# Two attentions on one Trainium2 core: where a step's eight value matmuls stand in TensorE's queue

## The chip, the cores and the metric

The kernel runs on one core of one Trainium2 chip. The metric is the device time of one execution in microseconds (us). A core has a matmul engine (PE, with its weight loads shown as PEld), a vector engine (DVE), a scalar engine (ACT), a general engine (POOL) and DMA queues, one of which is issued by SP. Each engine works through its own queue in the order written; between engines only semaphores order the work.

## The reference

What is computed is a chain of two blocks over x (2 batches, 1024 tokens, 128 channels). The change touches the two attentions with 16 heads of 8 channels over 1024 keys:

```python
attn = jnp.einsum('bhnd,bhmd->bhnm', q, k) * scale      # block 0
attn = jax.nn.softmax(attn, axis=-1)
attn_out = jnp.einsum('bhnm,bhmd->bhnd', attn, v)
...
p = jax.nn.softmax(qk, axis=-1)                          # block 1
mask = jnp.triu(jnp.ones((s, s), dtype=p.dtype), k=0)
p = p * mask
z = jnp.einsum('bhqk,bhkd->bhqd', p, v)
```

In block 1 the mask stands behind the softmax, so all 1024 keys count in the sum, and the masked probabilities are only left out of the product with v. Between and behind the attentions stand two windowed attention layers with their feed-forward parts, and a mixture of four experts run for four rounds; these are not touched.

## The kernel before

**Tiling.** One function, `attention` (L578), does both attentions; `causal` is False for block 0 and True for block 1. The 32 pairs of batch and head are worked on as 8 units of 4 heads. A unit has 2 halves of 512 queries, and a half has 8 steps, one for each tile of 128 keys: `LAST` = 128 steps `g` in each attention. In a step four heads are scored: `score` (L733) is a matmul of 50 rows by 512 queries into one of **three** PSUM banks (`st_bank[e % 3]`, L738 waits for the exponential three scores back); ACT takes the exponential of each into `probs` (L811, four buffers of four heads). `values` (L743) multiplies the four `probs` tiles of a step with v: four fp32 matmuls (L757), which the trace shows as eight instructions, into one bank over eight steps. It waits first for the last exponential of its step (L746).

**Maxima.** The softmax needs the largest score of each query before its scores are made. So 11 steps ahead (`LEAD`), `maximum` (L703) makes the same products with queries on the partitions, two matmuls of 512 into a ring slot of two banks, and DVE takes the maximum of the slot (L822). A step carries two such maxima, in four matmuls. There are two ring slots; slot n waits (`claim`, L698) until DVE is through with entry n-2. A score and the maximum matmul behind it use different halves of the PE's rows and run beside each other.

**Extras.** Once in eight steps the ring takes one more entry of each of two kinds. `rows` (L717, steps with g % 8 = 5) turns sixteen finished maxima to rows, which DVE casts (L837) after having split them (L827, L829) and SP writes into the operands. `turn` (L726, steps with g % 8 = 1, from g = 9) transposes the finished sums of a half. Before it, in the same step, ACT copies the value bank out (`take_sums`, L801 to L803) behind the step's first exponential, and the `values` of a half's first tile (issued in that same step) waits for this copy (L750). One extra entry changes which of the two slots the next maximum gets.

**Causal part.** In block 1 the key tiles that the diagonal crosses (64 of 128 steps: tiles 0 to 3 of the first half of a unit, 4 to 7 of the second) also need `probs` times a triangle. POOL makes it (`mask`, L889, L898) once the step's last exponential is done, and `values` ends with matmuls over it (L766) that wait for POOL (L763). Columns beyond the diagonal go by L760 instead of L757.

**The order of a step on PE** is written out by hand in L784 to L795. With S for a score, M0a, M0b, M1a, M1b for the four matmuls of the two maxima, and V for the values of the step before:

S0 M0a S1 M0b S2 M1a S3 M1b V extras

In the first 117 steps all of it is there; the last 11 have no maxima.

Of the kernel before, what the change touches and what calls it, by code (L numbers as in the profile page):

```python
# [577 lines left out]
def attention(nc, k, tag, scale, causal, operands, pool_aside=None):  # L578
# [23 lines left out]
    with ctx:  # L602
# [20 lines left out]
        def entries(g):  # L623

            out = []
            pair = g + LEAD
            if pair < LAST:
                out += [("max", 2 * pair), ("max", 2 * pair + 1)]  # L630
            if pair % SEQ_TILES == 0 and pair // SEQ_TILES - 1 < HALVES:
                out.append(("rows", pair // SEQ_TILES - 1))
            if g % SEQ_TILES == 1 and g > SEQ_TILES:
                out.append(("turn", g // SEQ_TILES - 1))
            return out
# [61 lines left out]
        def _(pe):  # L697
# [5 lines left out]
            def maximum(m, half):  # L703
                it, p, j, t = max_at(m)
                if half == 0:
                    buf = claim(("max", m))
                    if m % (2 * STEPS) == 0:
                        pe.wait_ge(loaded[it % RING], 16 * 4 * (it // RING + 1))
                buf = ring[number["max", m] % 2]
                mm = pe.matmul(buf[:, half * CHUNK:(half + 1) * CHUNK],  # L710
                               q_op[it % RING][at_rows(p, MAX_ROW), j, t * P:(t + 1) * P],
                               k_op[it % RING][at_rows(p, MAX_ROW), j, half * CHUNK:(half + 1) * CHUNK],
                               start=True, stop=True)
                if half:
                    mm.then_inc(ring_ready, 1)
# [17 lines left out]
            def score(g, i):  # L733
                it, half, t = g // STEPS, g // SEQ_TILES % 2, g % SEQ_TILES
                h = heads_of(g)[i]
                e, p, j = GROUP * g + i, h % 2, h // 2
                if e >= 3:
                    pe.wait_ge(exp_done, e - 2)  # L738
                pe.matmul(st_bank[e % 3], k_op[it % RING][at_rows(p, MAX_ROW + 2), j, t * P:(t + 1) * P],  # L739
                          q_op[it % RING][at_rows(p, MAX_ROW + 2), j, half * CHUNK:(half + 1) * CHUNK],  # L740
                          start=True, stop=True).then_inc(st_ready, 1)

            def values(g):  # L743
                it, half, t = g // STEPS, g // SEQ_TILES % 2, g % SEQ_TILES
                r = it % RING
                pe.wait_ge(exp_done, GROUP * (g + 1))  # L746
                if g % STEPS == 0:
                    pe.wait_ge(v_staged, it + 1)
                if t == 0 and g:
                    pe.wait_ge(evacuated, g // SEQ_TILES)  # L750
                first_tile, final = t == 0, t == SEQ_TILES - 1
                full = CHUNK if not causal else min(max(t - 4 * half, 0) * P, CHUNK)
                for j in range(GROUP):
                    out = out_bank[32 * j:32 * j + 32, :]
                    pr = probs[:, g % PB, j, :]
                    if full:
                        last = pe.matmul(out[:, 0:full], stage_v[r][:, t, j, :], pr[:, 0:full],  # L757
                                         start=first_tile, stop=final and full == CHUNK, skip_group_check=causal)
                    if full < CHUNK:
                        last = pe.matmul(out[:, full:CHUNK], only_ones[:, :], pr[:, full:CHUNK],  # L760
                                         start=first_tile, stop=final, skip_group_check=causal)
                if causal and 0 <= t - 4 * half < 4:
                    pe.wait_ge(masked, it * SEQ_TILES + t + 1)  # L763
                    at = (t - 4 * half) * P
                    for j in range(GROUP):
                        last = pe.matmul(out_bank[32 * j:32 * j + 32, at:at + P], stage_vo[r][:, t, j, :],  # L766
                                         diag[:, t % 2, j, :], start=False, stop=final, skip_group_check=True)
                last.then_inc(pv_done, 1)

            def extras(found):  # L770
                for kind, arg in found:
                    if kind == "rows":
                        rows(arg)
                    if kind == "turn":
                        turn(arg)
# [8 lines left out]
            for g in range(LAST):  # L784
                it, half = g // STEPS, g // SEQ_TILES % 2
                if g % SEQ_TILES == 0:
                    pe.wait_ge(m_rows[half], 32 * (it + 1))
                pair = g + LEAD
                for i in range(GROUP):
                    score(g, i)  # L790
                    if pair < LAST:
                        maximum(2 * pair + i // 2, i % 2)
                if g:
                    values(g - 1)
                extras(entries(g))  # L795
            values(LAST - 1)
            turn(HALVES - 1)
# [1259 lines left out]
```

## Time and profile before

| what | value |
|---|---|
| median of 3 runs | 1954.28 us (1953.3 to 1956.46) |
| the profiled execution | 1954.34 us |
| its span, first to last instruction | 1952.6 us |
| mean granted TensorE clock | 0.901 |
| PE busy | 1605.0 us (82%) |
| DVE busy | 1407.1 us (72%) |
| ACT busy | 1129.6 us (58%) |
| POOL busy | 604.3 us (31%) |
| exponentials L811 | 1024, 535.2 us, 602 ns each |
| maxima L822 | 512, 600.8 us, 1219 ns each |
| exponentials of block 0 | from 129.8 us to 461 us |
| exponentials of block 1 | to 1440 us |

The profiled execution is as good as the median. Busy time is a union of what the trace shows of an engine; a matmul's row shows about 0.38 us from its start to its modelled end, although the next one can start 0.22 us behind it, so PE looks busier than it is. For an order of queues the starts of instructions tell more than the busy shares: the prediction works from the starts.

### The profile page before, as it was taken

To read this page: it belongs to the slowest core of one execution; us is meant where nothing else is said; L and a number is where in the kernel's file an instruction comes from. 1 tells how busy PE (TensorE), PEld (TensorE's weight loads), DVE (VectorE), ACT (ScalarE), POOL (GpSimd) and SP (SyncE) were. 2 spreads that over 40 slices of the span, in tenths; PEclk is the share of its full clock that TensorE was granted. 3 is DMA by queue.
4 is the path that set the end of the run, shared out by engine and by line. 5 is a ranking of instruction groups with operands and counts; after the bars stand their busy time and mean duration, and the time that the engine had idled before them with its cause. 6 is when DMAs were issued, how large, how long until landed. Compare 5 with 4: busy or idle time off the path is not lost. (4 is left out here: it accounts for less than half of the span.)

```text
span 1952.6 us, 29634 instructions
## 1 busy us (share of the span) xinstructions
PE 1605.0 (82%) x11120; PEld 874.2 (45%) x11120; DVE 1407.1 (72%) x2091; ACT 1129.6 (58%) x2178; POOL 604.3 (31%) x494
## 2 busy tenths in 40 slices
PE   6279999997578885888771999999965998989997
PEld 4012222223356653566540233333324776767775
DVE  3499999992766456664443999999925787869787
ACT  3228888885466733667341477777742554545454
POOL 2550000001566424564002122222211353535354
PEclk8659999998699986899885799999987898989899
DMA  2410001001011100111004001110011000000000
GB/s 69 145 34 18 18 18 28 7 1 47 28 23 29 26 19 23 29 29 26 1 5 163 17 18 21 24 36 5 4 28 49 1 1 0 0 0 0 0 0 21
DMA packets 56776, 49.14 MB, mean 25 GB/s; under 512 B 37800, under 2 KB 41256, under 8 KB 56016
## 3 DMA queue, kind: packets, MB, share of 16 engines
q1 hardware_dynamic: 56016, 45.29, 8.8%
q10 hardware_dynamic: 576, 2.16, 0.3%
q8 instruction: 78, 1.28, 0.3%
q14 instruction: 42, 0.34, 0.1%
q0 software_dynamic: 64, 0.07, 0.0%
HBM read 24.34 MB, written 14.68 MB: 20 GB/s over the span
## 5 line engine op out<-in xcount | busy, mean ns | idle before, releaser
L811 ACT ACTIVATE att_probs<-psum 128x512 f32<-128x512 f32 x1024 | 535.2, 602 | 214.4 <-PE psum L739 213.7
L822 DVE TENSOR_REDUCE att_neg_max<-psum 128x1 f32<-128x1024 f32 x512 | 600.8, 1219 | 77.2 <-PE psum L710 71.4
L710 PE MATMUL psum<-att_k_op,att_q_op 48*128 48x512 bf16 x1024 | 350.9, 409 | 89.2 <-PEq L370 67.7
L739 PE MATMUL psum<-att_q_op,att_k_op 50*128 50x512 bf16 x1024 | 314.0, 387 | 19.2 <-ACT att_probs L811 19.0
L1831 ACT ACTIVATE moe_hidden<-psum,moe_b 128x512 f32<-128x512 f32 x256 | 168.9, 690 | 136.6 <-PE psum L76 116.1
L757 PE MATMUL psum<-att_probs,att_v 128*32 128x512 f32 (+2 forms) x1664 | 203.1, 558 | 2.9 <-ACT att_sums L803 2.8
L739 PEld LDWEIGHTS psum<-att_q_op,att_k_op 50*128 50x128 bf16 x1024 | 78.2, 94 | 250.8 <-ACT att_probs L811 187.6
L64 DVE CAST moe_hidden_high<-moe_hidden 128x512 fp32r<-128x512 f32 x256 | 149.0, 599 | 41.7 <-ACT moe_hidden L1831 41.7
L1860 POOL TENSOR_TENSOR moe_hidden_low<-moe_hidden,moe_hidden_high 128x512 fp32r<-128x512 f32 x64 | 107.0, 1672 | 203.3 <-DVE moe_hidden_high L64 203.3
L710 PEld LDWEIGHTS psum<-att_k_op,att_q_op 48*128 48x128 bf16 x1024 | 72.6, 95 | 213.7 <-DVE att_neg_max L822 120.7
L898 POOL TENSOR_TENSOR att_diag<-att_probs,att_triangle 128x512 f32<-128x512 f32 x64 | 81.4, 1272 | 269.0 <-PE psum L760 176.7
L69 DVE TENSOR_TENSOR moe_hidden_low<-moe_hidden,moe_hidden_high 128x512 fp32r<-128x512 f32 x192 | 130.4, 679 | 0.0
L74 PE MATMUL psum<-moe_cur_high,moe_w_high 128*128 128x512 f32 x256 | 107.5, 420 | 27.6 <-PEq L136 13.8
L1378 DVE TENSOR_REDUCE wl_mx<-psum 128x4 f32<-128x512 f32 x64 | 44.0, 688 | 116.1 <-PE psum L1179 116.1
L1296 ACT ACTIVATE wl_pr<-psum,wl_mx 128x128 f32<-128x128 f32 x256 | 73.2, 368 | 87.8 <-DVE wl_mx L1378 87.7
L1427 POOL TENSOR_TENSOR wl_qk<-wl_qk,wl_part 128x512 f32<-128x512 f32 x64 | 81.5, 1275 | 111.2 <-DVE wl_part L1361 111.1
L74 PE MATMUL psum<-moe_hidden_high,moe_w_high 128*128 128x512 f32 x256 | 112.5, 439 | 0.0
L75 PE MATMUL psum<-moe_cur_low,moe_w_high 128*128 128x512 f32 x256 | 105.5, 412 | 0.0
L76 PE MATMUL psum<-moe_cur_high,moe_w_low 128*128 128x512 f32 x256 | 105.5, 412 | 0.0
L76 PE MATMUL psum<-moe_hidden_high,moe_w_low 128*128 128x512 f32 x256 | 100.5, 393 | 0.0
L75 PE MATMUL psum<-moe_hidden_low,moe_w_high 128*128 128x512 f32 x256 | 99.9, 390 | 0.0
L1854 POOL TENSOR_TENSOR moe_cur<-moe_cur,moe_term 128x512 f32<-128x512 f32 x64 | 86.5, 1352 | 24.9 <-DVE moe_term L1923 24.1
(235 smaller groups left out, 2857.7 us busy)
## 6 DMA issues: line engine op xcount, KB each, us to landing
wl_v_shift<-wl_v SPq DMA_DIRECT2D x62, 128.0 KB, 2.3
att_q_op<-qk_parts SPq DMA_DIRECT2D x32, 192.0 KB, 3.2
att_k_op<-qk_parts SPq DMA_DIRECT2D x32, 192.0 KB, 4.2
qk_parts<-rot_hi SPq DMA_DIRECT2D x12, 256.0 KB
qk_parts<-plain_hi SPq DMA_DIRECT2D x12, 256.0 KB
qk_parts<-rot_mid SPq DMA_DIRECT2D x8, 256.0 KB
qk_parts<-plain_mid SPq DMA_DIRECT2D x8, 256.0 KB
moe_w<-in_moe_w SPq DMA_DIRECT2D x2, 1024.0 KB, 6.2
```

The lines of the kernel that those rows point to most:

```text
L64: return dve.tensor_copy(dst, src)
L69: return dve.tensor_tensor(dst, src, high.bitcast(F32), ALU.subtract)
L74: pe.matmul(out, w_high, x_high, start=start, stop=False)
L75: pe.matmul(out, w_high, x_low, start=False, stop=False)
L76: return pe.matmul(out, w_low, x_high, start=False, stop=stop)
L710: mm = pe.matmul(buf[:, half * CHUNK:(half + 1) * CHUNK], q_op[it % RING][at_rows(p, MAX_ROW), j, t * P:(t + 1) * P], k_op[it % RING][at_r ...
L739: pe.matmul(st_bank[e % 3], k_op[it % RING][at_rows(p, MAX_ROW + 2), j, t * P:(t + 1) * P], q_op[it % RING][at_rows(p, MAX_ROW + 2), j, ha ...
L757: last = pe.matmul(out[:, 0:full], stage_v[r][:, t, j, :], pr[:, 0:full], start=first_tile, stop=final and full == CHUNK, skip_group_check ...
L811: act.activation(probs[:, g % PB, h, :], st_bank[e % 3], ACT.Exp, scale=scale).then_inc(exp_done, 1)
L822: dve.tensor_reduce(neg[:, t, p, j:j + 1], ring[e % 2], AX.X, ALU.max, negate=True).then_inc(ring_free, 1)
L1831: act.activation(hidden[:, n % 2, f, :], k.psum[:, f, :], ACT.Gelu_apprx_tanh, bias=b1[:, e, f:f + 1]).then_inc(gelu_done, 1)
L1860: pool.tensor_tensor(hidden_low[:, n % 2, f, :], hidden[:, n % 2, f, :], hidden_high[:, n % 2, f, :].bitcast(F32), ALU.subtract).then_inc( ...
```

## The change

The `values` of the step before are issued behind the second score and its maximum matmul, instead of behind the fourth. Nothing else is changed; every wait, buffer and instruction is the same.

```diff
@@ -790,8 +790,8 @@
                     score(g, i)
                     if pair < LAST:
                         maximum(2 * pair + i // 2, i % 2)
-                if g:
-                    values(g - 1)
+                    if i == 1 and g:
+                        values(g - 1)
                 extras(entries(g))
             values(LAST - 1)
             turn(HALVES - 1)
```

The order of a step on PE is then: S0 M0a S1 M0b V S2 M1a S3 M1b extras. As the function is shared, it holds for both attentions.

## Rows read from the trace of the kernel before

**Rows 1.** The page, part 2: granted clock in 40 slices of the span.

```profile
PEclk8659999998699986899885799999987898989899
```

**Rows 2.** Busy by stretch: PE, PEld, DVE, ACT, POOL (instructions); clock, DMA share, GB/s.

```profile
290.00:310.00 20.00, 19.30 (x133) 4.94 (x134) 19.43 (x20) 16.55 (x33) 0.40 (x1) 1.00 0.16 41
```

**Rows 3.** Timeline of ACT, block 0: start, length, instructions, [idle before].

```profile
299.79 0.60 ACT L811 ACTIVATE att_probs<-psum 128x512 f32<-128x512 f32 x1 [0.33 <-PE psum L739]
300.28 0.59 ACT L803 ACTIVATE att_sums<-psum 128x512 f32<-128x512 f32 x1
...
303.02 2.06 ACT L811 ACTIVATE att_probs<-psum 128x512 f32<-128x512 f32 x4 [0.68 <-PE psum L739]
305.42 2.07 ACT L811 ACTIVATE att_probs<-psum 128x512 f32<-128x512 f32 x4 [0.33 <-PE psum L739]
307.81 2.06 ACT L811 ACTIVATE att_probs<-psum 128x512 f32<-128x512 f32 x4 [0.33 <-PE psum L739]
310.20 2.06 ACT L811 ACTIVATE att_probs<-psum 128x512 f32<-128x512 f32 x4 [0.33 <-PE psum L739]
...
318.17 2.06 ACT L811 ACTIVATE att_probs<-psum 128x512 f32<-128x512 f32 x4 [0.40 <-PE psum L739]
```

**Rows 4.** Timeline of PE, block 0, a step without extras.

```profile
306.07 0.39 PE L739 MATMUL psum<-att_q_op,att_k_op 50*128 50x512 bf16 x1
...
306.39 1.06 PE L757 MATMUL psum<-att_probs,att_v 128*32 128x512 f32 x8
307.39 0.39 PE L739 MATMUL psum<-att_q_op,att_k_op 50*128 50x512 bf16 x1
...
307.62 0.38 PE L710 MATMUL psum<-att_k_op,att_q_op 48*128 48x512 bf16 x1
...
308.08 0.39 PE L710 MATMUL psum<-att_k_op,att_q_op 48*128 48x512 bf16 x1
```

**Rows 5.** Timeline of DVE in the same step.

```profile
306.81 1.22 DVE L822 TENSOR_REDUCE att_neg_max<-psum 128x1 f32<-128x1024 f32 x1
...
308.06 2.36 DVE L822 TENSOR_REDUCE att_neg_max<-psum 128x1 f32<-128x1024 f32 x2
```

**Rows 6.** Timeline at block 0's end: last two exponentials, then the last values.

```profile
460.76 1.09 ACT L811 ACTIVATE att_probs<-psum 128x512 f32<-128x512 f32 x2
461.90 0.16 PEld L757 LDWEIGHTS psum<-att_probs,att_v 128*32 128x32 f32 x8 [0.99 <-ACT att_probs L811]
```

**Rows 7.** Timeline of PE, block 0: values in a turn step.

```profile
301.02 0.64 PE L757 MATMUL psum<-att_probs,att_v 128*32 128x512 f32 x4 [0.19 <-ACT att_sums L803]
```

**Rows 8.** Timeline of PE, block 0: M0a in the step behind a rows step.

```profile
313.16 0.39 PE L710 MATMUL psum<-att_k_op,att_q_op 48*128 48x512 bf16 x1 [0.40 <-DVE att_neg_max L822]
```

**Rows 9.** Timeline of PE, block 1: values with a diagonal part, then S0.

```profile
1269.07 0.87 PE L757 MATMUL psum<-att_probs,att_v 128*32 128x384 f32 x8
...
1269.96 0.42 PE L766 MATMUL psum<-att_diag,att_v 128*32 128x128 f32 x8
1270.31 0.39 PE L739 MATMUL psum<-att_q_op,att_k_op 50*128 50x512 bf16 x1
```

**Rows 10.** Timeline of ACT, block 1.

```profile
1266.43 1.09 ACT L811 ACTIVATE att_probs<-psum 128x512 f32<-128x512 f32 x2
...
1276.83 2.06 ACT L811 ACTIVATE att_probs<-psum 128x512 f32<-128x512 f32 x4 [0.57 <-PE psum L739]
1279.47 2.06 ACT L811 ACTIVATE att_probs<-psum 128x512 f32<-128x512 f32 x4 [0.57 <-PE psum L739]
```

**Rows 11.** Timeline of POOL, block 1: two of its 64 masks.

```profile
1267.61 1.28 POOL L898 TENSOR_TENSOR att_diag<-att_probs,att_triangle 128x512 f32<-128x512 f32 x1 [1.55 <-ACT att_probs L811]
...
1440.26 1.28 POOL L898 TENSOR_TENSOR att_diag<-att_probs,att_triangle 128x512 f32<-128x512 f32 x1 [1.37 <-ACT att_probs L811]
```

**Rows 12.** Timeline of PE, end of block 1: diagonal matmuls that wait for the mask.

```profile
1441.60 0.32 PE L766 MATMUL psum<-att_diag,att_v 128*32 128x128 f32 x4 [0.27 <-POOL att_diag L898]
```

**Rows 13.** Timeline of PE early in block 0, at the lower clock.

```profile
133.99 1.93 PE L757 MATMUL psum<-att_probs,att_v 128*32 128x512 f32 x8
```

## The prediction, made before the changed kernel was built

> **What bounds the kernel now.** I read the busy time by stretch first. In a stretch of block 0, DVE is busy 19.43 of 20 us and PE 19.30, ACT only 16.55 [rows 2]. By these shares DVE or PE is the bound and the order of PE's queue hardly matters. Then I read the starts, and they say something else. ACT begins a step of four exponentials every 2.39 us (305.42, 307.81, 310.20) and stands idle 0.33 us before each, waiting for a score [rows 3]. On PE, S3 starts at 306.07, V at 306.39, the next step's S0 at 307.39 [rows 4]. The chain that fills the period is: exponential 0 starts 305.42; S3 needs its bank (three banks) and starts 0.65 us later; V is queued behind S3 and M1b, 0.32 later; V holds the queue 1.00; S0 to its exponential takes 0.42 (307.39 to 307.81). 0.65 + 0.32 + 1.00 + 0.42 = 2.39. That is a **loop between ACT and PE**, and each link is a row. DVE does not close it: two of its maxima start 1.25 us apart where it had to wait for M0b (306.81, 308.06; M0b started at 307.62, 0.44 us earlier [rows 4]), while two that do not wait stand 1.14 apart (2.36 for two, less one length of 1.22 [rows 5]).
>
> **What the change does to a plain step.** Nothing is added or removed; V moves past S2, M1a, S3 and M1b. No DMA and no other queue's order moves. V's own wait, for exponential 3 of the step before, was long met when V came last; now it stands where it counts. S1 starts when exponential 2 of the step before has given its bank back. V could follow M0b by 0.32, but exponential 3 ends 0.48 after exponential 2 (four start within 2.06 less one length of 0.62, so 0.48 apart [rows 3]), so V always waits for ACT, about 0.15 us. Behind V stand S2 and S3. So the new loop is: exponential 3 starts; V starts 0.65 later (its length 0.60 and a hand-over of 0.05: the pair of exponentials that begins at 460.76 ends at 461.85, V's weights load at 461.90 [rows 6]); V holds PE 1.00 [rows 4]; S2 to exponential 2 takes 0.42 [rows 4, 3]; the next exponential starts 0.49 behind one that came late (299.79 to 300.28 [rows 3]). 0.65 + 1.00 + 0.42 + 0.49 = **2.56 us, 0.17 more than 2.39**. The old loop with V's wait taken out would be 0.65 + 0.32 + 1.00 + 0.42 = 2.39 again, so even a free wait gains nothing: V stands in front of two scores in place of four, yet ACT has only two in hand in place of three. The steps without maxima have the same loop. 128 steps in each block: +21.8 us in each.
>
> **A turn step (g % 8 = 1).** V now waits in mid-step for ACT's copy of the sums, which stands behind exponential 0. From the start T of exponential 3: exponential 0 at T + 0.48, the copy at T + 0.97, V 0.73 behind the copy's start (300.28 [rows 3], 301.02 [rows 7]), so T + 1.70 in place of T + 0.65: +1.05. The step is 3.61.
>
> **The step behind it.** One extra entry shifts the ring, so that M0a of the next step needs the slot that M1 of the turn step filled. M1b used to come before V, and its maximum was taken under V's 1.00 us. Now M1b is last, and only the extra and S0 stand between it and M0a. From M1b: 0.44 to DVE's start, 1.27 from there to the slot's release (306.81 [rows 5] to M1a at 308.08 [rows 4]), 0.22 to M0b, 0.32 to V: V starts 2.25 behind M1b. In a plain step M1b stands 1.87 behind T and the next V 2.56 + 0.65 behind T, 1.34 apart. So V loses another 0.92. That such a wait happens at all is seen today behind a rows step (0.40 us on DVE before M0a [rows 8]). The two steps together pay 1.05 + 0.92 = 1.97 for a turn. Today it costs 303.02 - 299.79 = 3.23, less 2.39, 0.84 [rows 3]. Net +1.12 for 15 turns in block 0, less 0.9 for the last, which has no maxima behind it: +15.9 us.
>
> **A rows step (g % 8 = 5).** The same slot wait falls on the step behind it: 0.92. The matmuls of `rows` themselves lie under it. Today three steps from 310.20 to 318.17 take 7.97 in place of 7.17: 0.80 [rows 3]. Net +0.12, 15 times: +1.8 us. DVE's load stays under it: 97% of 20.76 us (8 x 2.39 + 0.84 + 0.80), 20.2 us, in eight steps that now take 23.4 (8 x 2.56 + 1.97 + 0.92).
>
> Block 0: 21.8 + 15.9 + 1.8 = **39.5 us**.
>
> **Block 1, the mask.** In 64 steps V carries a diagonal part that waits for POOL. Today V comes so late that the mask is ready (POOL begins 1267.61, ends 1268.89 [rows 11]; the diagonal matmuls start 1269.96 [rows 9]). Such a step takes 2.64 now (1276.83 to 1279.47 [rows 10]). After: exponential 3 ends T + 0.60; POOL begins 0.08 later (1267.53, the end of the two exponentials [rows 10], to 1267.61) and takes 1.28; the hand-over to PE is 0.05 (1441.54 to 1441.60 [rows 11, 12]): T + 2.02. V's first part, begun at T + 0.65, takes 0.89 [rows 9] and is done at T + 1.54, so PE stands 0.48 us behind POOL. Then 0.35 of diagonal matmuls (1269.96 to 1270.31), 0.42 and 0.49 as above: **3.28 in place of 2.64, +0.64**. 64 x 0.64 = 41.0. The 64 others: 64 x 0.17 = 10.9. The extras in units' plain halves go as in block 0: 8 x (1.12 + 0.12) less 0.9 = 9.0. Those in diagonal steps I take at nothing: the late copy (V at T + 1.70) and the slot wait lie mostly under the mask wait (T + 2.02); if that cover is gone they cost up to 14 x 1 us more, and as they already cost up to 0.8 each today they could also give 5 back. Block 1: **60.9 us**.
>
> **Sum.** 39.5 + 60.9 = 100.4 us on the profiled execution's 1954.34, which stands at the median (1954.28): 2055 us. A difference of about 0.2% is what a measurement of this kernel can tell from no change. The terms I cannot read are bounded so. V's start behind a waited exponential: 0.05 after the end [rows 6], at most 0.14, as behind the copy (0.73 less 0.59 [rows 7, 3]); I take the first, which is the same wait; the other end adds 0.09 x 190, 17 us. The slot wait: 0.92 computed, none at best; it stands on some 42 steps (39 us) in the sum, and I take it whole as rows 8 show its kind; half of it is 19 us.
>
> **Rivals.** (a) **DVE sets the pace**: its work is unchanged, it is busy 97% [rows 2], so nothing changes: 1954. Against it: DVE's starts 1.25 apart where 1.14 is possible [rows 5], and the loop that adds up. The Trainium skill (Perfetto Trace Analysis, "Identifying the Most-Contended Engine") calls the engine with the highest occupancy the one to look at first; by that this would be the case, but the rows' starts disagree. 5%. (b) **Faster**: the extras (0.84 and 0.80 a half) come earlier against DVE, since rows and turns no longer queue behind V, and the step falls to DVE's floor, 20.2 us a half in place of 20.76; over 30 halves 17 us: 1937. It decides if V's wait for ACT is met on arrival and M1b's maximum is out of the slot before M0a. The first fails by 0.15, the second by 0.9 us. 4%. (c) **Only the mask hurts less**: POOL's 1.28 is covered after all and block 1 loses 0.17 a step: 100.4 - 64 x 0.47 = 70 us: 2025. For it: nothing but that other stalls can overlap. 6%. (d) **The clock falls**: in attention the granted clock is 1.00 [rows 2] (2.4 GHz); the page's slices show it lower elsewhere [rows 1]. At the lower level V is 1.93 in place of 1.06 long [rows 13, 4]; with that alone a step grows by 0.87, 256 steps 223 us: 2280. For it: PE gets new waits each step. Against: they are 0.15 to 0.5 us, and today's waits before S3 and M1a are like them at a clock of 1.00. The Trainium skill (TensorE: Matmul & The Clock Gate, "A second HAM failure mode: psum-queue depth-cycling") tells of a kernel where short idle times between groups of matmuls made the clock go up and down; this trace does not agree, its attention steps have such gaps and stay at 1.00. 2%.
>
> **Numbers.** My forecast 83%: 2055, its own range by the bounds 2055 - 19 - 5 to 2055 + 17: 2031 to 2072. The low end goes down to (c), the high end takes in a few of the 14 us of lost cover: 2025 to 2075. Faster 0.04, same 0.05, slower 0.91.
>
> **What would show it.** ACT's starts 2.56 apart in plain steps of block 0, with an idle of 0.5 before exponential 2 and not before exponential 0; V's weights waiting on L811; a turn pair 3.6 and 3.5 long; in block 1 L766 waiting about 0.48 on L898 in most of 64 steps, steps of 3.28; DVE no longer nearly full. It would be wrong if steps stay 2.39 (V's wait met), if M0a behind extras does not wait, or if the clock in the attentions is under 1.00.

## The result and the profile after

The changed kernel takes 2063.72 us (median of 4 runs, 2060.4 to 2064.29) where the kernel before took 1955.37 us beside it (1953.3 to 1959.49). The ratio is 1.0548, with a 95% interval of 1.0526 to 1.0569: **slower by 5.5%, some 108 us**. Forecast were 2055 us and a range of 2025 to 2075. All times and ratios here are of undisturbed executions; one of e6's four, at 2980.2 us, was a slow one and is left out.

The page of the changed kernel, in its parts 1, 2 and 5 (busy us, mean ns of one, then idle time before the group and what ended most of it):

```profile
span 2062.5 us, 29606 instructions
...
PE 1604.9 (78%) x11092; PEld 861.3 (42%) x11120; DVE 1413.4 (69%) x2091; ACT 1140.8 (55%) x2178; POOL 604.8 (29%) x494
...
PEclk9569999998589996999975899999997799999999
...
L822 DVE TENSOR_REDUCE att_neg_max<-psum 128x1 f32<-128x1024 f32 x512 | 608.2, 1220 | 182.2 <-PE psum L710 179.1
L811 ACT ACTIVATE att_probs<-psum 128x512 f32<-128x512 f32 x1024 | 546.6, 603 | 311.0 <-PE psum L739 309.6
```

The work is the same: PE busy 1604.9 us (1605.0 before), one exponential 603 ns (602), one maximum 1220 ns (1219). (ACT's busy time still shows 11 us more, 1140.8 for 1129.6: exponentials that follow without a wait start 0.48 us apart and are 0.60 long, so their rows overlap, and fewer now do.) What grew is waiting. ACT now stands idle 311.0 us in front of its exponentials, 214.4 before, and in nearly all of it for a score. DVE, which looked full, waits 182.2 us for maximum matmuls, 77.2 before.

The same stretch of block 0 as in [rows 2], by stretch (PE, PEld, DVE, ACT, POOL, then the clock):

```profile
290.00:310.00 20.00, 16.83 (x119) 4.27 (x119) 16.86 (x17) 14.61 (x29) 0.00 (x0) 1.00 0.01 1
```

PE and DVE fell from 97% to 84% together, at a clock of 1.00. So neither sets the pace of the changed kernel. That DVE did not set it before either is not shown by this; e11 below shows it.

ACT's timeline in block 0, changed kernel (start, length; a group of four now begins with a step's exponential 2, in front of which ACT waits):

```profile
304.11 2.07 ACT L811 ACTIVATE att_probs<-psum 128x512 f32<-128x512 f32 x4 [0.92 <-PE psum L739]
306.68 2.07 ACT L811 ACTIVATE att_probs<-psum 128x512 f32<-128x512 f32 x4 [0.49 <-PE psum L739]
309.24 2.07 ACT L811 ACTIVATE att_probs<-psum 128x512 f32<-128x512 f32 x4 [0.49 <-PE psum L739]
...
315.40 2.07 ACT L811 ACTIVATE att_probs<-psum 128x512 f32<-128x512 f32 x4 [0.92 <-PE psum L739]
...
320.53 1.58 ACT L811 ACTIVATE att_probs<-psum 128x512 f32<-128x512 f32 x3 [0.49 <-PE psum L739]
...
327.65 2.07 ACT L811 ACTIVATE att_probs<-psum 128x512 f32<-128x512 f32 x4 [0.92 <-PE psum L739]
```

304.11 to 306.68 to 309.24: a plain step is **2.56 us**, 2.39 before [rows 3]. A rows step and the next are 6.16 (309.24 to 315.40), a turn's two steps 7.12 (320.53 to 327.65).

PE's timeline in a plain step, changed kernel:

```profile
316.06 0.39 PE L739 MATMUL psum<-att_q_op,att_k_op 50*128 50x512 bf16 x1 [0.25 <-ACT att_probs L811]
...
316.55 1.06 PE L757 MATMUL psum<-att_probs,att_v 128*32 128x512 f32 x8
317.54 0.39 PE L739 MATMUL psum<-att_q_op,att_k_op 50*128 50x512 bf16 x1
...
319.11 1.06 PE L757 MATMUL psum<-att_probs,att_v 128*32 128x512 f32 x8
```

S1 at 316.06, V at 316.55, which is 0.49 later and not the 0.32 at which a V can follow (the rest is the wait for exponential 3), S2 at 317.54, the next V 2.56 behind. In the answer on waits for 150 to 470 us, V's weights waiting for ACT, 5.5 us in 150 to 430 us before, now stand high (third line: total us, times, longest):

```profile
PEld psum L739 <- ACT att_probs L811: 135.2, 205, 0.8
ACT att_probs L811 <- PE psum L739: 82.5, 149, 1.1
PEld psum L757 <- ACT att_probs L811: 58.3, 109, 1.4
```

Block 1, a diagonal step of the changed kernel, PE, POOL and ACT:

```profile
1290.57 0.66 PE L757 MATMUL psum<-att_probs,att_v 128*32 128x256 f32 x8
...
1291.95 0.43 PE L766 MATMUL psum<-att_diag,att_v 128*32 128x128 f32 x8 [0.28 <-POOL att_diag L898]
1292.30 0.39 PE L739 MATMUL psum<-att_q_op,att_k_op 50*128 50x512 bf16 x1
```

```profile
1290.59 1.30 POOL L898 TENSOR_TENSOR att_diag<-att_probs,att_triangle 128x512 f32<-128x512 f32 x1 [2.66 <-ACT att_probs L811]
```

```profile
1289.43 2.07 ACT L811 ACTIVATE att_probs<-psum 128x512 f32<-128x512 f32 x4 [1.17 <-PE psum L739]
1292.73 2.07 ACT L811 ACTIVATE att_probs<-psum 128x512 f32<-128x512 f32 x4 [1.23 <-PE psum L739]
```

V and the mask begin at the same time (1290.57, 1290.59); the mask ends at 1291.89 and the diagonal matmuls follow at 1291.95. The step is 3.30 us (1289.43 to 1292.73), 2.64 before [rows 10].

Between the starts of the first and the last exponential, the trace has block 0 at 374.3 us (331.4 before) and block 1 at 410.7 us (346.6 before): +42.9 and +64.1. What lies between the blocks took 3.3 us more in the profiled pair, although nothing changed there; over all the runs below it lies between 626.5 and 638.7 us (631.7 in the profile of before), so this is scatter. The kernel before itself, timed 13 times beside e4 to e6 and e8, gave 1949 to 1964 us.

### The profile page after: what moved, and what is told of

Its sections match the earlier page's. It is cut to its first block and busy times, and to the rows that moved or that the text cites. A ratio compares the mean times of both kernels' runs of the same rounds, so it can differ in the third digit from the quotient of the medians.

```text
span 2062.5 us, 29606 instructions
## 1 busy us (share of the span) xinstructions
PE 1604.9 (78%) x11092; PEld 861.3 (42%) x11120; DVE 1413.4 (69%) x2091; ACT 1140.8 (55%) x2178; POOL 604.8 (29%) x494
## 3 DMA queue, kind: packets, MB, share of 16 engines
q8 instruction: 78, 1.28, 0.3%
## 5 line engine op out<-in xcount | busy, mean ns | idle before, releaser
L822 DVE TENSOR_REDUCE att_neg_max<-psum 128x1 f32<-128x1024 f32 x512 | 608.2, 1220 | 182.2 <-PE psum L710 179.1
L811 ACT ACTIVATE att_probs<-psum 128x512 f32<-128x512 f32 x1024 | 546.6, 603 | 311.0 <-PE psum L739 309.6
L710 PE MATMUL psum<-att_k_op,att_q_op 48*128 48x512 bf16 x1024 | 335.7, 407 | 103.2 <-PEq L370 69.6
L739 PE MATMUL psum<-att_q_op,att_k_op 50*128 50x512 bf16 x1024 | 318.8, 388 | 44.5 <-ACT att_probs L811 44.4
L76 PE MATMUL psum<-moe_hidden_high,moe_w_low 128*128 128x512 f32 x256 | 100.4, 392 | 0.0
L760 PE MATMUL psum<-att_probs,att_only_ones 128*32 128x512 f32 (+3 forms) x768 | 84.1, 504 | 19.9 <-ACT att_sums L803 17.6
```

The lines of the kernel that those rows point to most:

```text
L76: return pe.matmul(out, w_low, x_high, start=False, stop=stop)
L710: mm = pe.matmul(buf[:, half * CHUNK:(half + 1) * CHUNK], q_op[it % RING][at_rows(p, MAX_ROW), j, t * P:(t + 1) * P], k_op[it % RING][at_r ...
L811: act.activation(probs[:, g % PB, h, :], st_bank[e % 3], ACT.Exp, scale=scale).then_inc(exp_done, 1)
L822: dve.tensor_reduce(neg[:, t, p, j:j + 1], ring[e % 2], AX.X, ALU.max, negate=True).then_inc(ring_free, 1)
```

## The experiments

The diffs show the lines that matter, against the kernel before; e10's is against e4. Block times are those between first and last exponential in the profiled execution; totals are medians. The ratios are estimates against executions of before made beside each run (medians 1955.3 to 1959.4 us) and need not be the quotient of two numbers of this table.

| run | block 0 | block 1 | total | ratio to before (95%) |
|---|---|---|---|---|
| before | 331.4 | 346.6 | 1955 to 1959 | 1 |
| changed | 374.3 | 410.7 | 2063.7 | 1.0548 (1.0526, 1.0569) |
| e1 block 0 only | 372.3 | 346.6 | 2000.5 | 1.0218 (1.0181, 1.0256) |
| e2 block 1 only | 331.6 | 409.5 | 2019.6 | 1.0315 (1.0275, 1.0354) |
| e3 lag two | 362.7 | 382.4 | 2027.9 | 1.0355 (1.0316, 1.0394) |
| e4 behind S0 | 455.9 | 499.8 | 2241.5 | 1.1465 (1.1396, 1.1535) |
| e5 behind S2, M1a | 404.8 | 416.5 | 2095.1 | 1.0708 (1.0668, 1.0748) |
| e6 extras behind V | 361.3 | 404.7 | 2043.6 | 1.0462 (1.0409, 1.0516) |
| e7 diagonal late | 372.3 | 382.2 | 2037.2 | 1.0420 (1.0383, 1.0458) |
| e8 before, diagonal split | 332.1 | 340.0 | 1949.8 | 0.9964 (0.9944, 0.9983) |
| e9 behind S2, before M1a | 361.5 | 384.6 | 2027.5 | 1.0363 (1.0327, 1.0399) |
| e10 e4 with filler | 457.6 | 498.4 | 2231.4 | 1.1389 (1.1353, 1.1425) |
| e11 values in halves | 317.8 | 342.2 | 1941.4 | 0.9922 (0.9898, 0.9946) |

**e1 and e2: one block at a time.** The values stand at `i == 1` in one block and last in the other.

```diff
-                if g:
+                    if i == 1 and g and not causal:   # e2: and causal
+                        values(g - 1)
+                if g and causal:                      # e2: and not causal
                     values(g - 1)
```

> Only block 0's attention has the values behind the second score; block 1 has the old order. My theory (each block's loop stands alone): block 0's exponentials take 374 us in place of 331, block 1 keeps its 374, the total is about 43 us over before, near 1998 us; the two one-block runs together give the whole change. Rival (something outside the attentions, such as the clock or the layers between, takes part): the two do not add up to 108 us, or a one-block run gains or loses in the other block.

> Only block 1's attention has the new order. My theory: block 1's exponentials take 438 us in place of 374, block 0 keeps 331, the total is about 64 us over before, near 2019 us. Rival: as for the block 0 run, the parts do not add up.

Measured: 45 us over before with block 0 alone, 64 with block 1 alone by the medians, together 109; by the ratios 43 and 62, together 104, each known to some 8 us. The whole change costs 107 to 108. The unchanged block keeps its time to 0.2 us in both. So the two costs stand apart and add up within what can be measured. (The 374 us that the expectations give block 1 before is not the 346.6 of the table; what they forecast is the differences, 43 and 64, and the block times show 41 and 63.)

**e3: the same place, but nothing to wait for.** The values are those of two steps before, the copy of the sums and the turns come one step later.

```diff
-                if g:
-                    values(g - 1)
+                    if i == 1 and g >= 2:
+                        values(g - 2)
...
+            values(LAST - 2)
             values(LAST - 1)
```

> The values stand in the new place but are those of two steps before (copy of the sums and turns one step later), so their wait for ACT and for POOL's mask is long met. My theory (what costs is V's wait for the last exponential, in front of S2 and S3): plain steps return to 2.39 us, diagonal steps to 2.64, only the copy's wait and the slot wait behind extras stay; per half about 1.9 us over before, some 2000 us in all. Rival (the place alone costs, since ACT has two scores in hand in place of three while V runs): plain steps stay at about 2.56, total near 2035. Second rival (with the wait gone the gap is filled): steps under 2.39, total under before.

ACT's timeline, e3:

```profile
304.98 2.06 ACT L812 ACTIVATE att_probs<-psum 128x512 f32<-128x512 f32 x4 [0.93 <-PE psum L739]
307.37 2.06 ACT L812 ACTIVATE att_probs<-psum 128x512 f32<-128x512 f32 x4 [0.33 <-PE psum L739]
```

Plain steps are back at 2.39 us and diagonal ones at 2.64: the 0.17 and the 0.64 were V's waits, and the place alone costs nothing in a plain step. Nor does it gain anything. The total came out 28 us over what I expected. Part of that is my sum: 1.9 us in each of some 30 halves make 57 us, near 2012 and not 2000. The rest is that the extras cost more than I had set: 22.86 us in eight steps of block 0 where 20.77 were taken before (2.1 over, for 1.9 expected), and in block 1 some 24.1 for 21.8 (2.3 over).

**e4, e5: other places.** `i == 0` and `i == 2` in place of `i == 1`.

> The values of the step before stand behind the first score and its maximum matmul, one place earlier than in the change. My theory gives the loop: 0.65 + 1.00 + 0.42 (S1 to exponential 1) + 0.49 + 0.48 = 3.04 us in a plain step, in a diagonal step 2.02 + 0.35 + 0.42 + 0.49 + 0.48 = 3.76; the total near 2158 us. Rival (the cost of the change is a matter of DVE's slots or of a fixed wait for ACT of about 0.17 that is paid once wherever V stands in front of a score): about the changed kernel's 2064.

Plain steps of e4 are 3.05 us (3.04 expected), diagonal ones 3.78 (3.76). So the sum of the loop extends to another place. But the total is 83 us over the expected: the extras cost far more (27.8 us in eight steps of block 0, of which 24.4 are plain), the clock fell 19 times in the two blocks, and plain steps at the end took 4.14 us each, see e10.

> The values stand behind the third score and its matmul. S2 itself waits for the last exponential of the step before, so V's wait is met when it comes. My theory: plain steps 2.39 us as before (0.65 + 0.32 + 1.00 + 0.42), diagonal steps 2.79 (V's first part is done at T + 1.86, the mask at T + 2.02), extras dearer than before by about 1 us a turn and 0.3 a rows step; the total near 1993 us. Rival (each place further forward costs alike): plain steps between 2.39 and 2.56, total near 2010 or over.

**A miss**: e5 takes 3.05 us a plain step, not 2.39, and is slower than the changed kernel. PE's timeline, e5:

```profile
302.41 0.39 PE L710 MATMUL psum<-att_k_op,att_q_op 48*128 48x512 bf16 x1 [0.28 <-DVE att_neg_max L822]
302.73 1.06 PE L757 MATMUL psum<-att_probs,att_v 128*32 128x512 f32 x8
...
303.73 0.60 PE L710 MATMUL psum<-att_k_op,att_q_op 48*128 48x512 bf16 x2
...
304.80 0.39 PE L739 MATMUL psum<-att_q_op,att_k_op 50*128 50x512 bf16 x1 [0.25 <-ACT att_probs L811]
305.46 0.39 PE L710 MATMUL psum<-att_k_op,att_q_op 48*128 48x512 bf16 x1 [0.28 <-DVE att_neg_max L822]
```

and DVE's:

```profile
304.18 1.22 DVE L822 TENSOR_REDUCE att_neg_max<-psum 128x1 f32<-128x1024 f32 x1 [0.70 <-PE psum L710]
```

S2 starts at 304.80 as forecast, but M1a stands until 305.46, when DVE gives back the slot that M1b filled at 303.73. A maximum whose first matmul stands in front of V and whose second stands behind it holds its slot for all of V. M1b to DVE 0.45, DVE to M1a 1.28, M1a to V 0.32, V to M1b 1.00: 3.05. That loop was in my rows all along (its first two links, 0.44 and 1.27, are those of the prediction's slot wait); I had closed it only behind extras. In e5's last steps, which have no maxima, the trace shows 2.39.

**e9: the maxima out of V's way.** V directly behind S2, in front of M1a.

```diff
                     score(g, i)
+                    if i == 2 and g:
+                        values(g - 1)
                     if pair < LAST:
                         maximum(2 * pair + i // 2, i % 2)
-                if g:
-                    values(g - 1)
```

> As the kernel with the values behind the third score (2095 us, plain steps 3.05), but V now stands directly behind S2, in front of M1a, so that no maximum has its first matmul before V and its second behind it. New theory (a ring slot that is claimed before V and filled behind it makes a loop of its own: V 1.00, M1b to DVE 0.44, DVE to the next M1a 1.27, M1a to V 0.32 = 3.04): the loop is gone, plain steps fall to 2.39 us, the diagonal steps to about 2.8, extras cost about 2 us more a half than before; near 2025 us. Rival (a V behind the third score is late for exponential 3 whatever the maxima do): plain steps stay at 3.05, near 2095.

ACT's timeline, e9:

```profile
304.34 2.07 ACT L811 ACTIVATE att_probs<-psum 128x512 f32<-128x512 f32 x4 [0.66 <-PE psum L739]
306.73 2.07 ACT L811 ACTIVATE att_probs<-psum 128x512 f32<-128x512 f32 x4 [0.33 <-PE psum L739]
```

2.40 us a plain step (304.34 to 306.73) and 2.81 a diagonal one, 2027.5 us in all for 2025 expected. One matmul's place is worth some 68 us here. Both loops, the one over ACT and the one over DVE's slots, are now shown one by one.

**e6: the slot wait behind extras.** In the changed kernel, `extras` stands behind the values at `i == 1`, and `entries` lists it between the step's two maxima.

```diff
+                    if i == 1:
+                        if g:
+                            values(g - 1)
+                        extras(entries(g))
```

> The changed kernel, but rows and turn stand behind the values in mid-step, also in the order of ring slots, so that M0a of the next step gets the slot that the extra used and no longer M1's. My theory (the slot wait costs 0.92 in the step behind each extra): a turn's two steps fall from 7.12 to about 6.76 us (the wait gone, but 0.59 of transposes now in front of S2), a rows step and the next from 6.17 to about 5.44; some 27 us less than the changed kernel, near 2037. Rival (the slot wait is not what holds V; the copy and the transposes are): no gain, or a loss of 0.59 a turn and 0.32 a rows step, near 2080.

ACT's timeline, e6 (a rows step and the next):

```profile
303.05 2.07 ACT L814 ACTIVATE att_probs<-psum 128x512 f32<-128x512 f32 x4 [0.49 <-PE psum L741]
...
308.67 2.07 ACT L814 ACTIVATE att_probs<-psum 128x512 f32<-128x512 f32 x4 [0.53 <-PE psum L741]
```

303.05 to 308.67 is 5.62 us (6.16 in the changed kernel), a turn's two steps 6.78 (7.12). Block 0 gains 13 us, block 1 six, the total 20 (17 by the ratios) of the 27 expected; some 5 us of the miss is the rows step, where I had expected 5.44. The transposes then stand in front of S2 and cost their 0.59; that the whole still gains shows that the slot wait was there, and the turn's 0.34 fits 0.92 - 0.59.

**e7: the diagonal part late.** In the changed kernel, the matmuls of L766 stand in a function `diagonal` behind M1b.

```diff
+                    if i == 1 and g:
+                        values(g - 1)
                 if g:
-                    values(g - 1)
+                    diagonal(g - 1)
```

> The changed kernel, but the diagonal part of the values stands alone behind M1b, so S2 and S3 no longer wait for POOL's mask. My theory: diagonal steps of block 1 fall from 3.29 to about 2.45 us (0.65 + 0.89 + 0.42 + 0.49), 64 times 0.84 = 54 us less than the changed kernel, near 2010. Rival (the diagonal part's own time and not POOL's is the cost): the matmuls are all still there, so it gains nothing or a few us, near 2060.

Diagonal steps fall from 3.29 to 2.59 us with all matmuls still there. The edit takes two things from in front of S2, the wait for POOL's mask and the diagonal matmuls' own 0.35 us, so e7 alone does not tell them apart. e3 does: there the mask is long done and the diagonal matmuls stand in their place, and the step is 2.64 again. Of the 0.64 over before, V's wait for ACT is 0.17 (as in plain steps) and the mask's wait the rest, some 0.47. The total gained 26 us, not 54. Diagonal steps that also have an extra gain little (of each 16 steps, five gain 0.6 to 0.7, one 0.2, and one loses 0.1), as the copy or the slot wait takes the mask's place. And the step is 2.59, not 2.45: I took 0.89 for V without its diagonal part, which is the distance to the start of the diagonal matmuls; a score right behind V starts 1.03 after it in this trace, and 0.65 + 1.03 + 0.42 + 0.49 = 2.59.

**e8: the diagonal part split off in the kernel before**, issued at `i == 1` of the step after; the values stay last.

```diff
+                    if i == 1 and g >= 2:
+                        diagonal(g - 2)
                 if g:
                     values(g - 1)
```

> The kernel before, with the diagonal part of block 1's values taken out of the values and issued in the middle of the step after the next score pair, where PE waits for ACT anyway. My theory of the loop (0.65 + 0.32 + V + 0.42): V is 0.89 without its diagonal part, so diagonal steps fall from 2.64 to about 2.35 us and the total by about 18 us, near 1937. Rival (PE's queue is full there, so the 0.35 us of matmuls cost the same wherever they stand): no change, 1955; or slower, if S2 behind them comes late for ACT.

ACT's and PE's timelines, e8, diagonal steps:

```profile
1279.02 2.06 ACT L824 ACTIVATE att_probs<-psum 128x512 f32<-128x512 f32 x4 [0.39 <-PE psum L739]
1281.48 2.06 ACT L824 ACTIVATE att_probs<-psum 128x512 f32<-128x512 f32 x4 [0.39 <-PE psum L739]
```

```profile
1278.60 0.39 PE L739 MATMUL psum<-att_q_op,att_k_op 50*128 50x512 bf16 x1
...
1279.14 0.42 PE L775 MATMUL psum<-att_diag,att_v 128*32 128x128 f32 x8
...
1280.03 0.87 PE L757 MATMUL psum<-att_probs,att_v 128*32 128x384 f32 x8
...
1281.05 0.39 PE L739 MATMUL psum<-att_q_op,att_k_op 50*128 50x512 bf16 x1
```

2.45 us, 2.64 before: block 1 falls by 6.6 us, the total by 0.36% (0.17 to 0.56). Less than the 18 us expected, for two reasons. The same mis-sized 0.89: with 1.02 (1280.03 to 1281.05) the loop is 2.41, where I had set 2.28. And the rival was partly right: from S0 (1278.60) by the diagonal matmuls (1279.14) and V (1280.03) to the next S0 (1281.05), PE issues one thing after another, 2.45 us without a wait in the trace. Its own queue is full in these steps, and the 0.35 us gain only what they take out of the loop.

**e10: the clock in e4's last steps.** e4, with one matmul added beside each score in the steps that have no maxima (shortened here; it waits until DVE is through with the last maximum):

```diff
                     if pair < LAST:
                         maximum(2 * pair + i // 2, i % 2)
+                    else:
...
+                        pe.matmul(ring[p][:, CHUNK:2 * CHUNK], q_op[...], k_op[...], start=True, stop=True)
```

> The kernel with the values behind the first score, whose last 10 steps in each block (without maxima) took 4.14 us at a granted clock of 0.50, not 3.05 at 1.00. Added: in those steps one matmul of 48 rows by 512 beside each score, into PSUM that nobody reads. Theory (PE was granted the lower clock because it did too little in those steps): with more PE work the clock stays at 1.00 there and the steps take 3.05 us, about 10 us less in each block, near 2220. Rival (those steps are longer for another reason, their different order of heads or the missing waits for DVE): they stay at 4.14 or grow with the added matmuls.

By stretch, the last steps of block 0, e4 and then e10:

```profile
560.00:587.00 27.00, 23.81 (x87) 3.41 (x79) 0.55 (x2) 12.90 (x25) 0.00 (x0) 0.50 0.00 0
```

```profile
565.00:587.00 22.00, 18.53 (x116) 4.37 (x114) 0.55 (x2) 14.58 (x29) 0.00 (x0) 1.00 0.01 1
```

ACT's timelines there, e4 and then e10:

```profile
574.17 2.06 ACT L811 ACTIVATE att_probs<-psum 128x512 f32<-128x512 f32 x4 [2.08 <-PE psum L739]
578.32 2.06 ACT L811 ACTIVATE att_probs<-psum 128x512 f32<-128x512 f32 x4 [2.08 <-PE psum L739]
```

```profile
574.34 2.07 ACT L817 ACTIVATE att_probs<-psum 128x512 f32<-128x512 f32 x4 [0.98 <-PE psum L739]
577.39 2.07 ACT L817 ACTIVATE att_probs<-psum 128x512 f32<-128x512 f32 x4 [0.98 <-PE psum L739]
```

In e4 the clock was at 0.50 (1.2 GHz) and a step took 4.14 us; in e10 PE got 1.00 (2.4 GHz) in spite of more to do, and the steps took 3.05. e4's own first three steps without maxima, still at 1.00, took 3.05 too, so the clock is what made the others long. As a gain it is small: in block 0, the ten steps after the maxima end took 35.4 us for 39.5, not the 10 us less expected, since the first added matmul had to wait for DVE and the clock fell there as well. Elsewhere in block 0 the clock happened to be at 0.50 for 63 us in e10 and 39 in e4, and the block as a whole took 457.6 us for 455.9. The totals, 2231.4 and 2241.5 us in two executions each, overlap (2228 to 2235, 2233 to 2250), so it is not shown that e10 is faster as a whole.

**e11: the values cut in two.** By queries: 256 behind M1b, the other 256 and the diagonal part one step later behind M0b, where everything they read is long done.

```diff
+                    if i == 1 and g >= 2:
+                        values(g - 2, 1)
                 if g:
-                    values(g - 1)
+                    values(g - 1, 0)
                 extras(entries(g))
+            values(LAST - 2, 1)
+            values(LAST - 1, 0)
+            values(LAST - 1, 1)
```

> The values are cut in two by queries (256 each): the first half stands behind M1b as in the kernel before, the second half (with block 1's diagonal part) one step later behind M0b, where its exponentials and its mask are long done. Nothing is left out. My theory (the loop exponential 0, S3, V, S0 is 0.65 + 0.32 + V + 0.42, and any V in the queue is paid only where it stands in the loop): with V of 0.50 the loop is 1.89, below ACT's 2.06 and DVE's 2.28, so plain steps fall from 2.39 to about 2.3 us, diagonal ones from 2.64 to about 2.4; some 30 to 40 us under the kernel before, near 1920. Rival (cutting doubles the weight loads and the gaps of 0.1 to 0.3 us between scores and values, so PE itself becomes the bound): no gain, 1955 or more.

PE's and DVE's timelines, e11, block 0:

```profile
304.14 0.64 PE L760 MATMUL psum<-att_probs,att_v 128*32 128x256 f32 x8
304.71 0.39 PE L739 MATMUL psum<-att_q_op,att_k_op 50*128 50x512 bf16 x1
...
305.25 0.64 PE L760 MATMUL psum<-att_probs,att_v 128*32 128x256 f32 x8
```

```profile
302.07 5.75 DVE L830 TENSOR_REDUCE att_neg_max<-psum 128x1 f32<-128x1024 f32 x5
```

A half V every 1.11 us, plain steps of 2.21 us, and five maxima in one piece without a wait, 1.13 apart. The loop over ACT is no longer the bound: PE issues scores and half values without a wait (0.57 from half V to a score, 0.23 to the next, 0.31 to the next half V), and DVE is busy 19.68 of the 20 us from 300 on. Block 0 takes 317.8 us, the total is 1941.4, 0.8% (0.5 to 1.0) under the kernel before, but 21 us over the 1920 expected. Block 1 gained 4.4 us only: its extras cost more than before (in 16 steps 5.2 us over the plain and diagonal ones, 3.3 before), and the clock fell five times there, at some 1.5 us each.

## Why the prediction was right

**The plain step** (2.56 forecast, 2.56 found) holds link by link, and e3, e4 and e9 show the loop by taking the wait away, by lengthening the path and by moving V. That a free wait would gain nothing is shown by e3. **The diagonal step** (3.28 for 3.29 to 3.30) is shown by e3 and e7. **The turn's two steps**: forecast 3.61 and 3.48, 7.09; found 3.64 and 3.48 from exponential 3 to exponential 3, 7.12. The slot wait, which I had computed and not seen in this form, is shown by e6, and the trace has it behind the rows step:

```profile
313.45 0.39 PE L710 MATMUL psum<-att_k_op,att_q_op 48*128 48x512 bf16 x1 [0.43 <-DVE att_neg_max L822]
313.46 0.39 PE L739 MATMUL psum<-att_q_op,att_k_op 50*128 50x512 bf16 x1
...
313.98 1.07 PE L757 MATMUL psum<-att_probs,att_v 128*32 128x512 f32 x8
```

The forecast sum, 100.4, was 8 us short of 108. The blocks' times hold 6.6 of the 8: block 0 grew by 42.9 for 39.5 forecast, block 1 by 64.1 for 60.9. **The rows step** was mis-sized: I forecast that step and the next at 2.56 + 3.48 = 6.04, they take 6.16. M1's slot comes free later than I had it, because DVE first splits the finished maxima (L827, L829): some 0.13 us, 15 times in block 0, 2 us. **The clock** was rival (d), and a small part of it came true. It fell three times in the attentions of the changed kernel, which it never did in those of before once they had left the 0.50 at which every attention starts: at 486.9 and 1531.3 us in the turn step among each block's last eleven, and at 1401.6 in a turn step with a diagonal part:

```profile
1401.70:1405.00 3.30, 3.30 (x24) 1.39 (x16) 0.68 (x1) 1.09 (x2) 0.00 (x0) 0.50 0.35 24
```

Each time cost about 1.2 us (the last turn step of block 0 and the next take 7.33 us in the changed kernel, 6.19 in e1, where the clock stayed), 3.5 in all, 1.1 of it in block 0 and 2.4 in block 1, which with the rows steps leaves less than 1 us over in each. What I wrote against it, that gaps like these were already there at a clock of 1.00, holds for plain steps; the turn step, where PE waits 1.17 us for the copy, was not covered by that. The longest wait of PE in before's attentions is 0.47 us. The changed kernel has 30 such waits of 1.17 us and three falls, so such a wait does not always bring one. The Trainium skill (TensorE: Matmul & The Clock Gate, "A second HAM failure mode: psum-queue depth-cycling"), which my text had set aside, tells of a clock that goes up and down with short idle times between groups of matmuls. The traces agree with that: e4 and e10, whose PE waits 0.9 us or more some 80 times, had 19 and 21 falls, the other runs none to five. The last 1.4 us of the 8 lie outside the attentions, within the scatter there.

Of the rivals, (a), that DVE sets the pace by its 97%, fell with the result, and with e11, where DVE does the same work in plain steps of 2.21 us and eight steps in 20.1 us for 20.8. (b) had two conditions, V's wait met on arrival and M1b's maximum out of the slot before M0a. e3 meets the first: its plain steps are 2.39, no shorter than before, and the second fails behind its extras. (c), a POOL mask that is covered, is wrong for diagonal steps without an extra. With a turn, two diagonal steps take 7.59 us (4.01 and 3.58), only 0.47 over the 7.12 of plain ones, an overlap that my sum already had.

That sum's account of extras in diagonal steps ("I take at nothing") held: in 16 steps of block 1 the changed kernel takes 8.0 us more, my terms give 7.7.

## What to carry to other kernels

Read the starts, not the shares: when two engines look 97% busy, add up the chain from one engine's start to the same start a period later, with each link from a row, and see which loop gives the measured period. A block of work that is moved forward in an in-order queue brings its waits with it, in front of everything it was moved past, and every buffer that is claimed before it and filled behind it is held for its whole length. If a long piece in such a queue is the problem, cutting it and spreading it (e11, 14 us under before) did more here than any place for the whole: every one tried in front of S3 was slower than the end of the step.

## What was not expected

- A V between the two matmuls of one maximum costs 0.65 us in each plain step (3.05 in e5, 2.40 in e9), by the place of one matmul that waits for nothing in itself.
- In the attentions, past their first steps, TensorE's clock fell only in steps with an extra or right behind one, after waits on PE of 0.4 us and more, and in e4's last steps. In e4, with 3.05 us steps, it stood at 1.00 in most of block 0, and in the last ones, without maximum matmuls, at 0.50. With added matmuls that nobody reads it was at 1.00 there, and the steps were shorter by 1.09 us. Even in e11, whose plain steps have no wait on PE, it fell five times, each time in a diagonal step behind a rows step.
- Sixteen matmuls of 256 columns took only 0.14 us longer than eight of 512: two halves at 0.57 us from V to the next score (304.14 to 304.71), against 1.00.
- If POOL is making a mask when DVE's small cast L827 starts, the cast takes 0.80 us in place of 0.18. It is held rather than slowed: in all seven such cases of before, and in the seven of the changed kernel (0.98 us), it ends 0.03 us after the mask does. In the profile of before, block 1:

```profile
1258.85 1.27 POOL L898 TENSOR_TENSOR att_diag<-att_probs,att_triangle 128x512 f32<-128x512 f32 x1 [22.13 <-PE psum L760]
```

```profile
1259.35 0.80 DVE L827 CAST att_neg_parts<-att_neg_max 128x16 bf16<-128x16 f32 x1
```
